# The front of a four-batch attention kernel reordered: gates ahead of query parts, piecewise stores, a folded scale

## What is computed

```
q, k, v, r = split(x_n @ W.T)                  # 128, 128, 128 and 16 columns
log_g = log_sigmoid(r);  log_G = cumsum over tokens
S = q k^T                                      # tokens t by s
P = S^2 * exp(log_G[t] - log_G[s]), causal     # up to one scale per row
y = (P v) / sum(P)
```

## Time and profile before

| | us |
|---|---|
| median of three runs | 556.91 |
| the three runs | 555.14, 556.91, 558.39 |
| the profiled execution, own time | 560.08 |
| the profiled execution, span | 558.3 |
| busy: PE, DVE, ACT, POOL | 443.8, 336.3, 334.8, 309.9 |
| scores of unit 0 start on TensorE | 40.59 |
| A of unit 0, of unit 9, of unit 79 start on VectorE | 45.0, 69.1, 229.6 |

### The profile page before, as it was taken

The page is one execution under the profiler, slowest core; times in us unless marked ns, Lnnn a source line. Parts: engine busy times, 40 slices in busy tenths (PEclk is TensorE's granted clock), DMA queues, the critical chain, the costliest instruction groups (busy, mean ns, idle before and its releaser), DMA issues. The chain is left out here.

```text
span 558.3 us, 11516 instructions
## 1 busy us (share of the span) xinstructions
PE 443.8 (79%) x3822; PEld 330.3 (59%) x3822; DVE 336.3 (60%) x804; ACT 334.8 (60%) x640; POOL 309.9 (56%) x333
## 2 busy tenths in 40 slices
PE   4485798878778577789888799895499896799990
PEld 2354476666656455568666577773277774577770
DVE  6659888967975898333571278646279738232211
ACT  2357699889886766745755456366167566245550
POOL 5215375564564235847636676642746872567771
PEclk9797699879889678799999979799599999699996
DMA  6334164254156820111321411112301122142224
GB/s 152 90 89 89 33 143 89 59 115 91 41 132 211 189 79 8 47 35 45 71 80 43 123 34 44 30 29 95 122 20 49 33 44 91 37 131 75 50 51 127
DMA packets 36515, 43.50 MB, mean 78 GB/s; under 512 B 5948, under 2 KB 31444, under 8 KB 36436
## 3 DMA queue, kind: packets, MB, share of 16 engines
q1 hardware_dynamic: 30572, 30.70, 20.9%
q0 software_dynamic: 5888, 12.07, 8.8%
HBM read 25.91 MB, written 15.86 MB: 75 GB/s over the span
## 5 line engine op out<-in xcount | busy, mean ns | idle before, releaser
L1450 POOL DMA_INDIRECT token_out<-ysb,id_out x92 | 93.5, 1016 | 81.5 <-ACT ysb L1609 63.4
L1088 POOL TENSOR_TENSOR PP<-PP,E 128x512 f32<-128x512 f32 x64 | 81.7, 1277 | 85.7 <-ACT PP L1038 85.5
L1669 DVE TENSOR_TENSOR hid<-silu,ps 128x352 f32<-128x352 f32 x92 | 47.8, 520 | 119.8 <-PE ps L1531 86.5
L1038 ACT ACTIVATE PP<-A,feps 128x1024 f32<-128x1024 f32 x80 | 92.7, 1158 | 23.5 <-DVE A L970 23.1
L970 DVE TENSOR_SCALAR A<-ps 128x1024 int32<-128x1024 int32 x80 | 96.3, 1218 | 14.9 <-PE ps L868 14.2
L1442 POOL DMA_INDIRECT tiled<-scaled_rows,id_in x92 | 90.3, 982 | 26.8 <-issue 21.8
L1510 ACT ACTIVATE turned<-ps 128x512 f32<-128x512 f32 (+2 forms) x104 | 56.9, 547 | 67.0 <-PE ps L1498 63.1
L1528 PE MATMUL ps<-room,turned 128*128 x184 | 78.2, 508 | 12.7 <-ACT silu L1602 10.5
L1544 PE MATMUL ps<-room,turned 128*128 x552 | 80.4, 283 | 4.1 <-ACT ysb L1609 3.9
L1544 PEld LDWEIGHTS ps<-room,turned 128*128 128x128 f32 x552 | 71.1, 197 | 6.2 <-issue 5.6
L1531 PE MATMUL ps<-room,turned 128*128 x184 | 73.8, 484 | 0.0
(11 more groups left out here) (222 smaller groups left out, 658.0 us busy)
## 6 DMA issues: line engine op xcount, KB each, us to landing
parts<-room SPq DMA_DIRECT2D x32, 128.0 KB, 2.4
scaled_rows<-xT SPq DMA_DIRECT2D x8, 512.0 KB, 2.6
yb<-token_out SPq DMA_DIRECT2D x8, 512.0 KB, 4.7
QS<-parts SPq DMA_DIRECT2D x21, 192.0 KB
KS<-parts SPq DMA_DIRECT2D x21, 192.0 KB
room<-in_L_ffn_w_dram SPq DMA_DIRECT2D x2, 1408.0 KB, 8.2
tiled<-scaled_rows,id_in POOLq DMA_INDIRECT x92, 2.7
token_out<-ysb,id_out POOLq DMA_INDIRECT x92, 2.4
```

The costliest lines, as they stand in the source:

```text
L1038: a.activation(PP[:, G % 2, 2 * p:2 * p + 2, :].rearrange("p k t -> p (k t)"), A[:, U % 3, :], ACT.Square, bias=feps[:, G // NG:G // NG + ...
L1088: g.tensor_tensor(w, w, E[:, hh % 4, :], MUL).then_inc(s_PD, 1)
L1450: g.indirect_dma_start(yr_d[m], bass.IndirectOffsetOnAxis(ap=id_out[:, m % 2, s:s + 1], axis=0), ysb[:, J % OUTS, :], None).then_inc(s_ret ...
L1669: v.tensor_tensor(hid[:, J % 2, 0:HID], silu[:, J % 2, :], ps[:, BK_B + J % 2, 0:HID], MUL).then_inc(s_hid, 1)
```

## The change

It has six edits.

1. **Order of VectorE.** The normalisations of batches 2 and 3 move up between the bounds of batch 0; batch 0's gate logs, totals and parts move ahead of most of its query parts (the queries' first cast stays ahead of them); batch 1's gate logs unit moves into the main loop, behind the A of unit 0, and `FRONT` shifts totals, parts, rows and differences one unit later. The wait for all values (`s_vz`) moves from ahead of the loop to behind unit 0's scores.
2. **Order of TensorE.** Batch 2's turn moves ahead of the gate sums; projections are split in two (`queries_keys_tensor`, `values_tensor`) so that the turn of batch 0's gates stands between batch 1's queries and values, and batch 1's bound steps around batch 3's queries and keys.
3. **Order of ScalarE.** The copies of turned blocks move ahead, and `decays_scalar(0)` from behind `gates_scalar(1)` to ahead of batch 3's copies.
4. **Stores.** Batch 0's pieces are stored as each is made, and the gates' store is issued without waiting for its landing there. The wait for the fills moves behind the first stores.
5. **Scale.** The multiplication of q by `fs` in place goes; the first cast takes q times `fs` straight to bfloat16, and the first subtraction becomes q times `fs` minus that piece. There are 8 steps for a batch in place of 9. For batches 2 and 3 ScalarE's cast takes the scale and the waits.
6. **Key rows.** For even groups, four transfers of one head become one transfer of four heads.

```diff
-        PARTS = 9
+        PARTS = 8
...
+            if G % 2 == 0:
+                heads = slice(GH * (G % NG), GH * (G % NG) + GH)
+                to = tiled[99:102, 4 * C:12 * C].bitcast(BF16).rearrange("k (r t) -> k r t", r=GH)
+                sp.dma_start(to, gates_d[b, 1, :, heads, :]).then_inc(s_keys[0], 16)
+                return
...
         def first_stack_sync():
             sp = nc.sync
+            sp.wait_ge(s_part, 1)
+            store_piece_sync(0, 1, 0)
+            store_piece_sync(0, 1, 3)
+            sp.wait_ge(s_part, 3)
+            store_piece_sync(0, 1, 1)
+            store_piece_sync(0, 1, 4)
             sp.wait_ge(s_part, 4)
-            store_sync(0, 1)
-            sp.wait_ge(s_store, 16 * 5)
+            store_piece_sync(0, 1, 2)
+            sp.wait_ge(s_part, 5)
+            store_piece_sync(0, 0, 0)
+            sp.wait_ge(s_fill, 64)
+            sp.wait_ge(s_store, 16 * 6)
             rows_of_sync(0, 0, 1, 0, GH, s_early)
+            sp.wait_ge(s_part, 7)
+            store_piece_sync(0, 0, 1)
             sp.wait_ge(s_part, PARTS)
-            store_sync(0, 0)
+            store_piece_sync(0, 0, 2)
+            gates_store_sync(0)
             sp.wait_ge(s_store, STORES)
             rows_of_sync(0, 0, 0, 0, GH, s_early)
-            gates_sync(0)
+            sp.wait_ge(s_gstore, 16)
             sp.dma_start(QS[96:99, 0, 0:8, :], gates_d[0, 0, :, 0:8, :]).then_inc(s_early, 16)
             keys_sync(0)
...
-            if n == 0:
-                v.tensor_scalar(qk[:, 0, b, :], qk[:, 0, b, :], fs[:, b:b + 1], None, MUL).then_inc(s_part, 1)
...
+                elif step == 0:
+                    ins = v.tensor_scalar(pt[:, 0, 0, :], qk[:, 0, b, :], scale, None, MUL)
...
+                elif step == 1:
+                    ins = v.scalar_tensor_tensor(rest[:, 0, :], qk[:, 0, b, :], scale, pt[:, 0, 0, :], MUL, SUB)
...
         def parts_scalar(b, step):
...
+            if step == 1:
+                a.wait_ge(s_store, STORES * (b - 1))
+                a.wait_ge(s_fs, bound_unit(b) + 1)
+                a.wait_ge(s_qk, 2 * b + 2)
...
+            elif n == 0:
+                a.activation(part[:, b % 2, 0, 0, :], qk[:, 0, b, :], ACT.Copy, scale=fs[:, b:b + 1]).then_inc(s_part, 1)
...
-        FRONT = {'totals': 0, 'parts': 1, 'rows': {2: 1, 3: 2, 4: 3}, 'differences': 5, 'clear': {1: 5, 3: 6},
+        FRONT = {'totals': 1, 'parts': 2, 'rows': {3: 1, 4: 2, 5: 3}, 'differences': 6, 'clear': {1: 5, 3: 6},
...
+                if hh == 0:
+                    pe.wait_ge(s_vz, B)
...
+                if U == FRONT['totals'] - 1:
+                    gate_logs_vector(1)
...
-                if 0 < b < B - 1 and k in (0, 3, 4, 7, 8):
+                if 0 < b < B - 1 and k in (3, 4, 7, 8):
                     parts_vector(b + 1, k)
...
@@ scalar
             gates_scalar(0)
             values_scalar(0)
-            for b in range(1, B):
-                proj_scalar(b)
-                values_scalar(b)
+            turn_scalar(0, 1, 1)
+            turn_scalar(0, 2, 0)
+            proj_scalar(1)
+            values_scalar(1)
+            turn_scalar(0, 3, 1)
+            proj_scalar(2)
+            values_scalar(2)
+            decays_scalar(0)
+            proj_scalar(3)
+            values_scalar(3)
             gates_scalar(1)
-            decays_scalar(0)
             heads_scalar()
@@ tensor
-            proj_tensor(0)
+            queries_keys_tensor(0)
+            values_tensor(0)
             turn_first_tensor(1)
             bound_turn_tensor(0)
             bound_spread_tensor(0)
+            turn_first_tensor(2)
             gate_sums_tensor(0)
-            proj_tensor(1)
-            turn_first_tensor(2)
+            queries_keys_tensor(1)
             gate_turn_tensor(0)
-            proj_tensor(2)
+            values_tensor(1)
             turn_first_tensor(3)
-            proj_tensor(3)
+            queries_keys_tensor(2)
+            values_tensor(2)
             bound_turn_tensor(1)
+            queries_keys_tensor(3)
             bound_spread_tensor(1)
+            values_tensor(3)
             heads_tensor()
@@ vector
             bound_vector(0, 0)
+            norm_apply(0, 2)
             bound_vector(0, 1)
+            norm_apply(0, 3)
             bound_most_vector(0)
             first_parts_vector(0, 1)
+            gate_logs_vector(0)
             bound_scale_vector(0)
-            first_parts_vector(0, 0)
-            norm_apply(0, 2)
-            gate_logs_vector(0)
+            first_parts_vector(0, 0, range(1))
             gate_totals_vector(0)
             gate_parts_vector(0)
+            first_parts_vector(0, 0, range(1, 4))
             gate_rows_vector(0)
-            norm_apply(0, 3)
             gate_differences_vector(0)
             bound_vector(1, 0)
             bound_vector(1, 1)
+            bound_most_vector(1)
             first_parts_vector(1, 1)
-            bound_most_vector(1)
             bound_scale_vector(1)
             first_parts_vector(1, 0)
-            gate_logs_vector(1)
             heads_vector()
```

More of the change, by code:

```diff
@@ L443, in keys_sync, with gates_store_sync @@
                 sp.wait_ge(s_D, GH * (G - 1))
+            if G % 2 == 0:
[3 more added lines that the diff above has]
+                return
             for r in range(GH):
-                sp.dma_start(gate_keys(G, r, slice(99, 102)), gates_d[b, 1, :, GH * (G % NG) + r, :]).then_inc(s_keys[G % 2], 16)
+                sp.dma_start(gate_keys(G, r, slice(99, 102)), gates_d[b, 1, :, GH * (G % NG) + r, :]).then_inc(s_keys[1], 16)
         def gates_sync(b):
+            sp = nc.sync
+            gates_store_sync(b)
+            sp.wait_ge(s_gstore, 16 * (b + 1))
+        def gates_store_sync(b):
             sp = nc.sync
@@ L450, in gates_sync, with store_piece_sync @@
             sp.dma_start(gates_d[b].rearrange("n k h t -> (k h) n t"), gk[:, b]).then_inc(s_gstore, 16)
-            sp.wait_ge(s_gstore, 16 * (b + 1))
+        def store_piece_sync(b, which, k):
+            nc.sync.dma_start(parts_d[b % 2, which, :, k, :, :], part[:, b % 2, which, k % 3, :]).then_inc(s_store, 16)
         def store_sync(b, which):
             for k in range((3, 5)[which]):
-                nc.sync.dma_start(parts_d[b % 2, which, :, k, :, :], part[:, b % 2, which, k % 3, :]).then_inc(s_store, 16)
+                store_piece_sync(b, which, k)
         def rows_of_sync(b, slot, which, first, n, done):
@@ L582, in turn_first_tensor, with queries_keys_tensor @@
             turn_tensor(0, b, b % 2)
-        def proj_tensor(b):
+        def queries_keys_tensor(b):
             pe = nc.tensor
@@ L594, in proj_tensor, with values_tensor @@
                           start=True, stop=True).then_inc(s_qkp, 1)
+        def values_tensor(b):
+            pe = nc.tensor
             if b:
@@ L746, in bound_scale_vector, with first_parts_vector @@
             v.tensor_scalar(feps[:, first:last], own, LOG_EPS, None, MUL).then_inc(s_fs, 1)
-        def first_parts_vector(b, n):
+        def first_parts_vector(b, n, steps=range(4)):
             v = nc.vector
@@ L752, in first_parts_vector @@
             done = PARTS * b + (0 if n else 4)
-            if n == 0:
-                v.tensor_scalar(qk[:, 0, b, :], qk[:, 0, b, :], fs[:, b:b + 1], None, MUL).then_inc(s_part, 1)
[L755 to L763, removed]
+            scale = fs[:, b:b + 1]
+            for step in steps:
+                if step:
+                    v.wait_ge(s_part, done + step)
+                if step == 0 and n == 1:
+                    ins = v.tensor_copy(pt[:, 1, 0, :], qk[:, 1, b, :])
+                elif step == 0:
+                    ins = v.tensor_scalar(pt[:, 0, 0, :], qk[:, 0, b, :], scale, None, MUL)
+                elif step == 1 and n == 1:
+                    ins = v.tensor_tensor(rest[:, 1, :], qk[:, 1, b, :], pt[:, 1, 0, :], SUB)
+                elif step == 1:
+                    ins = v.scalar_tensor_tensor(rest[:, 0, :], qk[:, 0, b, :], scale, pt[:, 0, 0, :], MUL, SUB)
+                elif step == 2:
+                    ins = v.tensor_copy(pt[:, n, 1, :], rest[:, n, :])
+                else:
+                    ins = v.tensor_tensor(pt[:, n, 2, :], rest[:, n, :], pt[:, n, 1, :], SUB)
+                ins.then_inc(s_part, 1)
         def parts_vector(b, step):
@@ L1907, in _ @@
             fill_sync()
-            sp.wait_ge(s_fill, 64)
             first_stack_sync()
```

34 lines of the change are left out of this document (15 added, 19 removed).

## The result

The changed kernel took 549.16 us (median of 4, 547.12 to 550.02) against 556.02 (median of 4 of the kernel before): ratio 0.9878, interval [0.9838, 0.9917], 6.8 us. On another chip, with more executions, the ratio was 0.9903 [0.9877, 0.9928], 5.4 us by that ratio. The forecast was 548.8, a gain of 8.1. Its direction, mechanism and size hold, but three terms of the sum were off, and the table further down shows how far.

What follows compares the result with a forecast made beforehand. No single engine bounds the kernel; what counts is when the loop reaches its pace. Unit 9 comes 8.9 us earlier, less 0.8 for TensorE's clock, gain 8.1: 556.9 to 548.8, range 545.5 to 553.5.

Steps and rivals of the forecast that it cites:

- normalisations moved into idle time: VectorE's front: two normalisations moved up fill idle time before 16.80; 0.3 us lost if they fit badly.
- low clock in the front: TensorE's clock around batch 1's projection: staying high costs nothing, falling costs 2.1 us; 0.8 taken.
- load and decays off ScalarE's path, z to E: ScalarE to the first E: 6.0 us less one table load of 1.28 and batch 0's decays of 0.32.
- scores wait for transfers: Sync queue: transfers land by 32.2 to 32.7, unit 0's scores start near 32.5, with 2 to 3 us of cover.
- E of unit 0, no collision, clock up: ScalarE's first E in the main loop, before any clock cost: starts at 35.8 rather than 45.23.
- unit 2 behind E of unit 0: First loop units: E at 35.8, then differences, mask, sums, totals and clearing put unit 2 at 40.7.
- unit 2 to unit 9: First loop units: 18.17 us before, plus 1.4 for gate parts moving in; unit 9 at 60.3.
- the scale, batches 0 and 1: VectorE's front: dropping the in-place query multiplication saves one operation, 0.5 us, for each batch.
- Rival 2: Units 2 to 9 or the loop stretch, another 6 us given back: gain 2, 555; chance 0.08.
- rival 3: TensorE's clock falls more often in the loop; 23 us more at low gives 559.6; chance 0.04.
- Rival 1: TensorE's clock falls in the front, costing the full 2.1: gain 6.8, 550.1; chance 0.15.
- rival 4: A ScalarE table load costs 1.4 us more than its row, a drain: gain 9.5, 547.4; chance 0.03.

Runs made afterwards that it cites:

- pool_early: Changed kernel with GpSimd's key-row memsets moved ahead of its last normalisation root; ratio 0.9751 to the kernel before, on chip C.
- warm: Changed kernel plus eleven useless matmuls in TensorE's gaps around batch 0's bound and ahead of its gate sums; ratio 0.9798 to the kernel before.
- early_warm: Changed kernel plus both the early key-row memsets and the eleven useless matmuls; 546.14 us against 555.41 for the kernel before, ratio 0.9831.
- pool_early2: Same kernel as pool_early, run again on chip B; 547.03 us, ratio 0.9844 to the kernel before.
- scale_back: Changed kernel with the queries again multiplied by their scale in place, as its own step, in front and loop; ratio 0.9911 to the kernel before.
- decays_back: Changed kernel with batch 0's decays back behind the gates of batches 1 to 3 on ScalarE; ratio 0.9892 to the kernel before.

## Why the prediction was right, and where its terms were off

| term | forecast | measured |
|---|---|---|
| normalisations moved into idle time | 0, at most 0.3 | 1.5 at the gate logs (pool_early), 1.0 to 1.4 at E |
| low clock in the front | 0.8, bounds 0 and 2.1 | at E: 1.85 (warm), 2.3 (early_warm against pool_early2), 2.4 (the two runs of pool_early) |
| load and decays off ScalarE's path, z to E | 1.6 (6.0 to 4.4) | 1.6 (6.01 to 4.41) |
| scores wait for transfers | E sees none, landing 32.2 to 32.7 | none that E sees; landing 32.7 (pool_early) |
| E of unit 0, no collision, clock up | 35.8 | 35.70, 35.57, 35.59 |
| unit 2 behind E of unit 0 | 4.9 | 3.67; 4.72 in pool_early |
| unit 2 to unit 9 | 19.6 | 19.8 |
| the scale, batches 0 and 1 | 0.5 each in VectorE's list | nothing seen at E |
| unit 9 earlier | 8.1 | 6.6; 7.0 counted from the first bound |
| total | 8.1 | 6.8, again 5.4 |

*What bounds the kernel.* Right, and shown by undoing: neither engine alone, but the order in which the lists wait for one another. A shift at unit 9 arrives at the end roughly whole. On chips A and B, unit 9 earlier by 1.1, 2.2, 6.9, 7.7, 7.9, 8.0, 9.3 and 10.3 us, by the table above, went with 0.7, 2.2, 5.4, 4.9, 8.7, 8.3, 9.4 and 9.4 us of time (the ratio's share of the kernel before). The changed kernel and scale_back kept less than the rest. Rival 2, that the gain does not arrive, falls, and so does rival 3: the mean clock of the loop was 0.86 before and 0.88 after, and none of the kernels was slower.

*The steps that failed.* "The two normalisations moved up fill idle time before 16.80": they did fill it, but GpSimd's memsets stood there. Beside the reductions of before they had disturbed nothing (0.69 each); beside the normalisations they stretched 1.1 us to 2.75, and the forecast had looked at VectorE's idle time alone. And "I take 0.8, nearer to staying high, because the idle is a fifth of the one seen": the clock fell with idles of at most 1.41 in the first run of the changed kernel and 1.89 in the second. Rival 1 had the right mechanism and nearly the size (2.1 against 1.85 to 2.4). It was given 0.15, and it happened. By unit 9 it and the collision together had cost less than at E, because TensorE's clock was up when the sums of unit 1 came, and unit 2 followed E after 3.67 and not 4.9. The first row is the changed kernel's, the second pool_early's, where it was down:

```profile
40.10 0.48 PE L639 MATMUL ps<-lg,tri 128*128 128x192 f32 x2
...
37.18 0.85 PE L640 MATMUL ps<-lg,tri 128*128 128x192 f32 x2
```

That return of 1.2 us is luck, as far as the forecast goes: it came in both runs of the changed kernel, but no term of the sum holds it, and in pool_early, pool_early2, warm and decays_back unit 2 followed after 4.7. Without it the gain at unit 9 would have been about 5.8 and not 7.0 (an estimate from these two numbers). And 6.8 is the gain that rival 1 had named; the time itself, 549.16, lies so near 548.8 because the kernel before measured 556.02 beside it and not the 556.91 that the forecast started from.

*The table loads.* The load of Exp moved as forecast, and rival 4 falls: the load at 37.70 ends 0.02 before E, and moving one ahead, under batch 3's projection, brought 1.6 with the decays, not 3.0.

*One transfer of four heads* for four was on no path that a run shows; it was not tried alone.

## What to carry to other kernels

When two engines run lists in order, a moved step is worth what the other list can do with it: here the change without VectorE's order kept 1.1 of 7 us at unit 9, and without TensorE's 2.2. Before filling a VectorE gap, look at what GpSimd does in it: four scalings of 128x128 took 2.75 us beside a memset and 1.11 without it, and a cast and a tensor_tensor were stretched beside GpSimd's products, while reductions beside the memset were not. And a gap that has become short need not give TensorE its full clock back: read the granted clock of the stretch. Useless matmuls held it here and brought about 2 us at E, but their worth in the total was not resolved.

## What was not expected of the hardware

TensorE's granted clock fell in one of two executions of the same kernel, on two chips, at the same place (1.94 and 3.73 for the same four matmuls), with no idle over 1.41 us, and stayed up in the one profiled execution of each of the three kernels with the eleven useless matmuls. A memset of 3 partitions by 2048 bfloat16 took 1.83 us, one of 96 by 1024 float32 0.95: the three partitions cost more than the ninety-six. And one of three chips took 6% longer for the same kernel (the kernel before, 590.21 against 554.86 and 555.41); in pool_early, the kernel profiled there and on another chip, the first 219 us agree to 0.5.
